# Every second feed-forward of an eight-batch sandwich kernel one step later, with halved rotary products and split preparation waits

## The chip, the cores and the metric

The kernel runs on one core of one Trainium2 chip. The metric is the device time of one execution in microseconds (us), from the first to the last instruction and what lies around it. A profiled execution gives, beside it, the span and what each engine did in it: TensorE (PE, matrix products; PEld its weight loads), VectorE (DVE), ScalarE (ACT), GpSimd (POOL) and SyncE (SP), which here issues the transfers.

## The reference

Eight batches x of 512 tokens by 256 features go through four sub-layers, each with a norm ahead and a norm behind it:

```python
x = x + _layernorm(_L0_attn_ref(_layernorm(x), ...))   # causal attention, 16 heads of 16,
...                                                    # plus one rotary score of 32 common to all heads
x = x + _layernorm(_L0_ffn_ref(_layernorm(x), ...))    # ternary weights, relu squared, hidden 1024
x = x + _layernorm(_L1_attn_ref(_layernorm(x), ...))   # "mixer": cumulative sums of p_w*cos, p_w*sin
x = x + _layernorm(_L1_ffn_ref(_layernorm(x), ...))    # relu, hidden 1024
```

with, in the first attention,

```python
k_rope = _rotary_apply(c_kv @ W_k_rope, cos, sin)
q_rope = _rotary_apply(x @ W_q_rope, cos, sin)
scores = jnp.einsum('bqhd,bkhd->bhqk', q, k)
scores = scores + jnp.einsum('bqr,bkr->bqk', q_rope, k_rope)[:, None]
```

and the ternary weights of the first feed-forward prepared from the latent ones (mean of absolute values, rounding, clipping, a low-rank product added).

## The kernel before, in words

All work of a batch is on one core and the batches overlap. Each engine has its own program, put together from named items. An item is a step such as S (a tile of scores), T (transposes of exponentials), fc (one of 8 products into the hidden layer of the first feed-forward) or gather (products that pick and add mixer terms). The items stand in four chains: a, attention of batches 0 to 7; d, the dense work (first feed-forward `fc`, `fproj`; the mixer's projections `z`, `query`; the mixer's output product `oout`; second feed-forward `gc`, `gproj`); m, the mixer (turn, frac, fold, cos, sin, scan, mix, gather, gate, silu); p, the preparation of weights, once.

Within a chain the order is that of `chains()`; across chains it is written out for each engine in `MERGE`, whose words say how many items of which chain come next (`a8 p a2` is eight of a, one of p, two of a). `PARTS` says which items an engine takes part in. Engines meet by semaphores only: `is_filled` and `is_drained` for banks of PSUM, `need` for other events. An engine that waits holds up all that stands behind it in its own order.

In chain d, for batches 1 to 7, `first_dense_items(b)` is followed by `second_dense_items(b - 1)`, and inside the latter, between gc and gproj, stand the norm and transposes (`head_items(b + 1)`: fstats, fnorm, fxT) of the first feed-forward of the next batch. The short name g(b) is used here for the second feed-forward of batch b: gstats, gnorm, gxT, gc, gproj, gystats, gsum. The banks of PSUM are planned from the orders (`plan_banks`): attention rotates over banks 0 to 2, chain d over 4 to 6, bank 3 is for PV (the product of weights and values), 7 for the mixer's sums and the preparation.

Where the steps are in the code of the profile: on TensorE S is L922, T L930, PV L948, OT (transposes of attention's output) L957, the general `product` L865 (fc with weights wfc, gc with wf, z, query, q, k, rotary qr with wqr and kr with wkr, and `base`, the rotary scores, shown as 32*128), `tokens_out` L875 (out with wo, oout with wout, fproj with wpr, gproj with wf and hid), `half_transposes` L857 (fxT, zxT, gxT), gather L1016, prep L1054 to L1075. On VectorE: drains of scores L1410, rotation L1340, L1341 and L1344, scan L1487, mix L1496, sums x + norm L1332, silu L1505, drains of gproj L1518. On ScalarE: exponentials L1176, copies L1183, statistics (`spread`) L1119, `gsum` scaling L1263, `normed` L1110, cosine and sine L1243 and L1246. On GpSimd: the reciprocal square roots L746, squares of the hidden layer L766, the last sum L786, and ternary weights L803 to L818. On SyncE: the store of the result L728, loads of ratios for the mixer L718.

Buffers that bear on the order: `xnd` holds the normed input of each dense part, and is also where statistics throw their unused output; `x3` holds x + oout and then the result, until it is stored (semaphore `stored`, awaited by osum L1508); `means` keeps the means of four batches.

## Time and profile before

| what | value |
|---|---|
| median of 3 runs | 1410.93 us (1410.14 to 1413.29) |
| the profiled execution | 1407.21 us, its span 1405.4 us |
| granted TensorE clock, mean of the span | 0.949 |
| TensorE busy | 1227.4 us, 87% |
| VectorE busy | 1101.7 us, 78% |
| ScalarE busy | 1054.7 us, 75% |
| GpSimd busy | 336.7 us, 24% |
| chain that ended last, by engine | PE 46%, DVE 21%, ACT 19%, issue 9% |

Busy is time with an instruction under way. A line of the timeline gives the start, the duration of a group of like instructions on that engine, the engine, the line of code, the operation, what is written and read, the tile (128*32 is 128 rows by 32 columns of TensorE) and the count; in brackets stands idle time before it and what ended that. The stretches in the first group of rows are cut at the starts of `out` of batches 0 to 7 (the last product of an attention), and, behind 1171.8, at 1261.4 and at the start of `oout` of batch 7.

### The profile page before, as it was taken

How to read it: one execution, taken by the hardware profiler on the slowest of the kernel's cores; microseconds unless marked ns; L12 is line 12 of the kernel's file. 1: busy time of each engine (PE TensorE's matmuls, PEld its weight loads, DVE VectorE, ACT ScalarE, POOL GpSimd, SP SyncE). 2: the span in 40 equal slices, each digit the busy share in tenths (PEclk: the TensorE clock that was granted, in tenths of full speed). 3: DMA queues.
4: the chain of work that ended last, by engine and by line, in shares of the span. 5: the costliest groups of instructions: out<-in, count | busy, mean ns of one | idle time of the engine just before them, and what ended most of it. 6: DMA issues, size and time to landing. Idle time of an engine off the chain costs nothing.

```text
span 1405.4 us, 22661 instructions
## 1 busy us (share of the span) xinstructions
PE 1227.4 (87%) x7820; PEld 774.3 (55%) x7820; DVE 1101.7 (78%) x2259; ACT 1054.7 (75%) x2107; POOL 336.7 (24%) x317
## 2 busy tenths in 40 slices
PE   5889987888899998999999997998999998874767
PEld 2565664364546565666646764565646755542444
DVE  3683358779988988988888997898788998998940
ACT  4784789689789878798778888597778889547532
POOL 3943203400121303220134001430032201511021
PEclk9799999999999999999999999999999999996879
DMA  8404114412252105520334131511352131103000
GB/s 260 99 13 101 28 24 137 108 50 61 70 135 61 31 1 150 130 53 1 124 80 107 24 100 45 136 31 24 108 124 57 31 92 47 45 19 126 23 16 15
DMA packets 72019, 101.49 MB, mean 72 GB/s; under 512 B 10641, under 2 KB 44065, under 8 KB 71905
## 3 DMA queue, kind: packets, MB, share of 16 engines
q1 hardware_dynamic: 71904, 100.03, 27.2%
q8 instruction: 64, 1.05, 0.3%
q14 instruction: 51, 0.41, 0.1%
HBM read 74.31 MB, written 25.69 MB: 71 GB/s over the span
## 4 chain that ended last, share of the span: by engine, by line
PE 46%; DVE 21%; ACT 19%; issue 9%; DMA 2%; SPq 2%; POOL 1%; DVEq 0%; POOLq 0%; ACTq 0%
PE ps L865 15%; PE ps L875 12%; DVE work L1487 8%; PE ps L930 5%; ACT work L1176 5%; ACT work L1183 3%; PE ps L922 3%; PE ps L948 3%; DVE work L1410 3%; PE ps L1016 3%; DVE work L1496 2%; DVE work L1478 2%; ACT xnd L1119 2%; DVE work L1468 1%; PE ps L857 1%
## 5 line engine op out<-in xcount | busy, mean ns | idle before, releaser
L1487 DVE TENSOR_TENSOR_SCAN work<-work 128x512 f32<-128x512 f32 x256 | 313.2, 1254 | 23.0 <-ACT work L1243 21.0
L1410 DVE CUSTOM_DVE_ANT_0 work<-ps,work 128x384 f32<-128x384 f32 (+3 forms) x512 | 228.9, 486 | 109.9 <-PE ps L922 106.5
L1176 ACT ACTIVATE work<-work 128x384 f32<-128x384 f32 (+3 forms) x512 | 264.4, 560 | 44.9 <-DVE work L1410 44.1
L746 POOL TENSOR_TENSOR later_norms<-later_norms,singles 128x2 f32<-128x2 f32 x112 | 97.0, 867 | 711.6 <-ACT xnd L1119 428.5
L930 PE MATMUL ps<-ident,work 128*128 128x128 f32 x1280 | 202.4, 284 | 23.7 <-ACT work L1183 11.0
L930 PEld LDWEIGHTS ps<-ident,work 128*128 128x128 f32 x1280 | 152.6, 145 | 82.5 <-issue 33.5
L1183 ACT COPY work<-ps 128x512 f32<-128x512 f32 x300 | 170.9, 576 | 8.6 <-PE ps L930 8.3
L1496 DVE TENSOR_TENSOR work<-work 128x1024 f32<-128x1024 f32 x128 | 160.7, 1255 | 4.0
L922 PE MATMUL ps<-work 96*128 96x384 bf16 (+3 forms) x512 | 124.8, 311 | 29.9 <-ACT work L1183 28.0
L865 PE MATMUL ps<-led_xTd,wfc 128*128 128x512 f32 x256 | 122.3, 615 | 0.8 <-ACT led_xTd L1103 0.8
L875 PE MATMUL ps<-wf,hid 128*128 128x256 f32 x512 | 114.1, 383 | 5.5 <-issue 5.5
L875 PE MATMUL ps<-wpr,hid 128*128 128x256 f32 x512 | 114.7, 383 | 4.1 <-POOL hid L766 4.1
L865 PE MATMUL ps<-led_xTd,wf 128*128 128x512 f32 x256 | 115.8, 609 | 1.4 <-issue 1.4
L875 PEld LDWEIGHTS ps<-wf,hid 128*128 128x128 f32 x512 | 97.6, 192 | 21.2 <-issue 8.0
L875 PEld LDWEIGHTS ps<-wpr,hid 128*128 128x128 f32 x512 | 97.1, 192 | 19.2 <-POOL hid L766 5.9
L766 POOL TENSOR_TENSOR hid<-hid 128x512 f32<-128x512 f32 x64 | 79.9, 1258 | 111.7 <-ACT hid L1198 111.5
L1478 DVE SCALAR_TENSOR_TENSOR work<-work,smalls 128x512 f32<-128x512 f32 x128 | 97.3, 804 | 6.0 <-ACT work L1234 3.6
L948 PE MATMUL ps<-work 128*32 128x128 f32 x2560 | 93.4, 284 | 0.4 <-ACT work L1183 0.4
L922 PEld LDWEIGHTS ps<-work 96*128 96x128 bf16 x512 | 43.1, 99 | 84.2 <-ACT work L1183 40.4
L1239 ACT ACTIVATE work<-work 128x1024 f32<-128x1024 f32 x64 | 67.2, 1058 | 26.1 <-DVE work L1478 25.9
L865 PEld LDWEIGHTS ps<-led_xTd,wf 128*128 128x128 f32 x256 | 49.2, 195 | 64.4 <-issue 63.7
L1016 PE MATMUL ps<-work,sel 128*32 128x512 f32 x512 | 63.1, 610 | 19.1 <-DVE work L1496 18.9
(174 smaller groups left out, 1967.4 us busy)
## 6 DMA issues: line engine op xcount, KB each, us to landing
work<-values SPq DMA_DIRECT2D x64, 256.0 KB, 3.3
work<-ratios SPq DMA_DIRECT2D x64, 256.0 KB, 3.3
scratch<-work SPq DMA_DIRECT2D x32, 384.0 KB, 4.5
work<-scratch SPq DMA_DIRECT2D x64, 192.0 KB, 3.9
work<-scratch SPq DMA_DIRECT2D x64, 128.0 KB, 4.2
x_in<-x SPq DMA_DIRECT2D x8, 512.0 KB, 7.0
work<-scratch SPq DMA_DIRECT2D x64, 64.0 KB, 4.3
values<-work SPq DMA_DIRECT2D x16, 256.0 KB, 2.8
```

Of the source, the lines that this page charges most:

```text
L865: i = mm(dst, l, r, start=j == 0, stop=j == len(pairs) - 1)
L875: i = mm(ps[:, bank(b, name), t * D:(t + 1) * D], lhs[:, j, tt * P:(tt + 1) * P], rhs[:, j, :], start=j == 0, stop=j == n_k - 1)
L922: i = mm(out_of(b, name)[:, at:at + nk], stack[0:SROWS, hg % 2, 0, j, qt * P:(qt + 1) * P], stack[0:SROWS, hg % 2, 1, j, 0:nk], start=True ...
L930: i = tr(ps[:, bank(b, name), t * P:(t + 1) * P], sc[:, n % 4, t * P:(t + 1) * P], ident[:])
L948: i = mm(ps[32 * j:32 * j + 32, PV, qt * P:(qt + 1) * P], v_all[:, v0:v0 + 32], pt[:, (hg * UNITS + u) % 6, at + t * P:at + (t + 1) * P], ...
L1016: i = mm(ps[l * W:(l + 1) * W, bank(b, f"mem{quad}"), :], sel[:], ring[:, at, m, :], start=half == 0 and m == 0, stop=half == 1 and m == M ...
L1176: i = s_.activation(part_of, part_of, ACT.Exp, scale=-1.0, bias=nmax[:, row:row + 1])
L1183: s_.copy(pt[:, n % 6, 0:nk], out_of(b, name)[:, 0:nk]).then_inc(*drains(b, name))
L1410: i = v_.tensor_tensor_reduce(sc[:, n % 4, at:at + nk], out_of(b, name)[:, at:at + nk], base_of(qt), -SCORE_SCALE, BIG, ALU.add, ALU.min, ...
L1478: i = v_.scalar_tensor_tensor(ring[:, SIN_HALF[r], m, :], kvr[:, slot, :], turns[:, r, m:m + 1], whole[:, COS_HALF[r], m, :], ALU.mult, AL ...
L1487: v_.tensor_tensor_scan(ring[:, at, m, :], pwr[:, slot, :], ring[:, at, m, :], 0.0, ALU.mult, ALU.add).then_inc(*scanned.one)
L1496: v_.tensor_tensor(both, both, qc[:, half * MH:(half + 1) * MH], ALU.mult).then_inc(*mixed.one)
```

## The change

It has three parts, and a new order of merging (`MERGE`) for all five engines.

*The second feed-forward one step later.* `oout`, its statistics and sums leave `second_dense_items` and become `output_items`. From batch 2 on, chain d is first(b), second(b-2), output(b-1), where it was first(b), second(b-1) with the output at its head. The end is second(6), output(7), second(7). `head_items(b + 3)` goes with it. On ScalarE `gystats` throws its output into `zc`, and so waits for the saved values of batch b+2; `fstats` and `fystats` wait for events of batch b-3 instead of b-2; `means` keeps all eight batches. In TensorE's order, attention 7 ends (`out(7)`) with g(0) to g(3), and the transposes and gc0, gc1 of g(4), done ahead of it. Behind it come the rest of g(4), oout(5), fc to query of batch 7, g(5), oout(6), g(6), oout(7), g(7), with the gathers of the last two mixers among them.

*Halved rotary products.* qr and kr use four column groups of 32 (two halves of the tokens, each with and without the swap), with 256 columns for each instruction. The rotation of q then has 256 elements on 64 partitions, that of k keeps 512 on 64. `base` of the later half is two products.

*Preparation.* The loads are split: the first prepare steps and the ternary weights wait for five of them (`loaded_raw`), the rest for all. In the order prep 8 to 12 are among the scores of attention 0, and 13 to 15 stand ahead of `out(0)` (before: behind `out(0)`, the last of them after kr of batch 1). Dense work starts sooner: fxT of batch 0 directly behind kr of batch 1, six fc of batch 0 ahead of its first score (before: three), and z and query of batch 0 some eight score tiles sooner.

```diff
 def second_dense_items(b):
 
-    return (steps(b, ["oout", ("oystats", 0), ("oystats", 1), ("osum", 0), ("osum", 1), ("gstats", 0), ("gstats", 1), ("gnorm", 0),
-                       ("gxT", 0), ("gnorm", 1), ("gxT", 1)] + [("gc", g) for g in range(HC)]) + head_items(b + 2) +
+    return (steps(b, [("gstats", 0), ("gstats", 1), ("gnorm", 0),
+                       ("gxT", 0), ("gnorm", 1), ("gxT", 1)] + [("gc", g) for g in range(HC)]) + head_items(b + 3) +
             steps(b, [("gproj", 0), ("gystats", 0), ("gsum", 0), ("gproj", 1), ("gystats", 1), ("gsum", 1)]))
+def output_items(b):
+
+    return steps(b, ["oout", ("oystats", 0), ("oystats", 1), ("osum", 0), ("osum", 1)])
...
-    for b in range(1, B):
-        dense += first_dense_items(b) + second_dense_items(b - 1)
+    dense += first_dense_items(1) + output_items(0) + head_items(2)
+    for b in range(2, B):
+        dense += first_dense_items(b) + second_dense_items(b - 2) + output_items(b - 1)
+    dense += second_dense_items(B - 2) + output_items(B - 1)
...
-                    product(b, "qr", out_of(b, "qr")[0:2 * DR],
-                            [(wqr[:, c].rearrange("p s r -> p (s r)"), xa_c[c]) for c in range(DC)])
+                    may_fill(pe, b, "qr")
+                    for c in range(DC):
+                        for g in range(4):
+                            h = g % 2
+                            i = mm(out_of(b, "qr")[g * DR:(g + 1) * DR, 0:T // 2], wqr[:, c, g // 2, :],
+                                   xa_c[c][:, h * T // 2:(h + 1) * T // 2], start=c == 0, stop=c == DC - 1)
+                    i.then_inc(*fills(b, "qr"))
...
-                    product(b, "kr", out_of(b, "kr")[0:2 * DR], [(wkr[:].rearrange("p s r -> p (s r)"), ckv)])
+                    may_fill(pe, b, "kr")
+                    for h in range(2):
+                        for g in range(4):
+                            of = (h + g) % 2
+                            i = mm(out_of(b, "kr")[g * DR:(g + 1) * DR, h * T // 2:(h + 1) * T // 2], wkr[:, g // 2, :],
+                                   ckv[:, of * T // 2:(of + 1) * T // 2], start=True, stop=True)
...
-                    product(b, f"base{n}", out_of(b, f"base{n}")[:, 0:(n + 1) * P],
-                            [(qrope[0:DR, n * P:(n + 1) * P], krope[0:DR, 0:(n + 1) * P])])
+                    name, h = f"base{n}", n // 2
+                    may_fill(pe, b, name)
+                    queries = qrope[h * DR:(h + 1) * DR, n % 2 * P:(n % 2 + 1) * P]
+                    if h == 1:
+                        mm(out_of(b, name)[:, 0:T // 2], queries, krope[DR:2 * DR, T // 2:T], start=True, stop=True)
+                    first, n_key = h * T // 2, (n % 2 + 1) * P
+                    i = mm(out_of(b, name)[:, first:first + n_key], queries, krope[h * DR:(h + 1) * DR, 0:n_key],
+                           start=True, stop=True)
...
                 if n == 0:
-                    pe.wait_ge(loaded, 16 * n_rest[0])
+                    pe.wait_ge(loaded_raw, 16 * n_raw[0])
...
                     if b and n == 0:
-                        is_filled(act, *((b - 2, "gxT1") if b > 1 else (0, "zxT1")))
+                        is_filled(act, *((b - 3, "gxT1") if b > 2 else (b - 1, "zxT1")))
...
                     is_drained(act, b, f"gproj{n}")
-                    spread(2, n, lambda t: xnd[:, t, :], x2[:, b % 2], o_stats)
+                    need(act, kv_saved[1], min(b + 2, B - 1), 1)
+                    spread(2, n, lambda t: xnd[:, t, :], zc[:, 1].rearrange("p (t d) -> p t d", t=2), o_stats)
...
-            def rotate(b, name, dst):
+            def rotate(b, name, dst, n):
+
                 is_filled(dve, b, name)
-                v_.tensor_tensor(rtmp[0:DR, 0, :], out_of(b, name)[0:DR], rope[0:DR, :], ALU.mult)
-                v_.tensor_tensor(rtmp[0:DR, 1, :], out_of(b, name)[DR:2 * DR], rope[DR:2 * DR, :], ALU.mult
+                v_.tensor_tensor(rtmp[0:2 * DR, 0, 0:n], out_of(b, name)[0:2 * DR, 0:n], rope[0:2 * DR, 0:n], ALU.mult)
+                v_.tensor_tensor(rtmp[0:2 * DR, 1, 0:n], out_of(b, name)[2 * DR:4 * DR, 0:n], rope[2 * DR:4 * DR, 0:n], ALU.mult
                                  ).then_inc(*drains(b, name))
```

## Rows read from the trace of the kernel before

**Rows 1.** Stretches: length, then busy (xcount) of PE, PEld, DVE, ACT, POOL; clock.

```profile
0.00:104.40 104.40, 81.64 (x667) 54.23 (x668) 65.00 (x224) 67.16 (x146) 64.47 (x57) 0.89 0.47 125
104.40:228.20 123.80, 113.06 (x809) 73.52 (x808) 60.12 (x196) 88.12 (x195) 24.32 (x29) 0.97 0.26 61
228.20:377.60 149.40, 122.94 (x848) 74.83 (x849) 126.81 (x260) 121.32 (x229) 31.14 (x28) 0.93 0.30 77
377.60:534.60 157.00, 145.25 (x966) 92.78 (x965) 134.70 (x275) 130.11 (x260) 33.20 (x33) 0.98 0.27 67
...
1009.90:1171.80 161.90, 152.39 (x998) 97.86 (x996) 143.05 (x291) 136.59 (x278) 36.60 (x36) 0.98 0.32 86
1171.80:1261.40 89.60, 78.11 (x319) 46.77 (x319) 82.63 (x87) 56.56 (x103) 24.96 (x20) 0.96 0.09 28
1261.40:1351.80 90.40, 54.29 (x198) 29.79 (x196) 77.39 (x82) 55.13 (x89) 7.92 (x8) 0.82 0.20 65
1351.80:1405.40 53.60, 38.09 (x120) 24.90 (x120) 3.14 (x6) 16.74 (x42) 7.82 (x9) 0.82 0.04 15
```

**Rows 2.** TensorE timeline around the end of attention 7: start, us, work.

```profile
1159.13 3.62 PE L875 MATMUL ps<-wout,work 128*128 128x256 f32 x16
...
1168.54 0.66 PE L857 MATMUL ps<-ident,xnd 128*128 128x128 f32 x4 [1.06 <-ACT xnd L1110]
...
1175.69 13.90 PE L865 MATMUL ps<-led_xTd,wf 128*128 128x512 f32 x32
1191.66 1.92 PE L1016 MATMUL ps<-work,sel 128*32 128x512 f32 x16 [2.07 <-DVE work L1496]
...
1196.14 13.98 PE L875 MATMUL ps<-wf,hid 128*128 128x256 f32 x64
```

**Rows 3.** TensorE timeline, tail.

```profile
1292.45 1.93 PE L1016 MATMUL ps<-work,sel 128*32 128x512 f32 x8 [13.33 <-DVE work L1496]
...
1351.82 6.21 PE L875 MATMUL ps<-wout,work 128*128 128x256 f32 x16 [4.36 <-DVE work L1505]
```

**Rows 4.** ScalarE, GpSimd and store queue behind gproj1 of batch 5 (timeline).

```profile
1211.23 0.51 ACT L1119 ACTIVATE x<-xnd,singles 128x256 f32<-128x256 f32 x1 [1.08 <-DVE xnd L1518]
...
1213.14 1.09 ACT L1263 ACTIVATE xnd<-xnd,means,later_norms 128x256 f32<-128x256 f32 x2 [0.82 <-POOL later_norms L746]
...
1214.31 1.79 POOL L786 TENSOR_TENSOR x<-x,xnd 128x512 f32<-128x512 f32 x1 [1.20 <-ACT xnd L1263]
...
1211.76 4.77 SPq L728 DMA_DIRECT2D out<-x  x2
```

**Rows 5.** TensorE timeline: rotary products; transposes ahead of PV and ahead of z.

```profile
21.98 1.93 PE L865 MATMUL ps<-xTa,wqr 128*64 128x512 f32 x4
...
25.75 1.07 PE L865 MATMUL ps<-work,wkr 128*64 128x512 f32 x2
...
1133.60 0.66 PE L930 MATMUL ps<-ident,work 128*128 128x128 f32 x4
1134.19 1.09 PE L948 MATMUL ps<-work 128*32 128x128 f32 x32
...
1135.44 0.60 PE L930 MATMUL ps<-ident,work 128*128 128x128 f32 x4
1135.88 1.45 PE L865 MATMUL ps<-led_xTd,wz 128*128 128x512 f32 x3
```

**Rows 6.** VectorE rotation by line: ns min, median, max; then a 256-element operation.

```profile
L1340 DVE TENSOR_TENSOR work<-ps,rope x16: 668/670/679, 24.0 to 1035.5; 32x512 f32<-32x512 f32 x16
...
L1344 DVE TENSOR_TENSOR work<-work x16: 679/826/1299, 25.4 to 1036.9; 32x512 f32<-32x512 f32 x16
...
L1424 DVE TENSOR_TENSOR xna<-ps,work 128x256 f32<-128x256 f32 x32 | 13.6, 425 | 1.1
```

**Rows 7.** TensorE timeline; VectorE waits, 104.4 to 228.2: total, times, longest.

```profile
28.79 0.76 PE L1054 MATMUL ps<-ident,work 128*16 128x128 f32 x4 [1.96 <-DMA b2r<-b]
...
DVE work L1410 <- PE ps L922: 46.7, 26, 11.7
```

49 lines of the change are left out of this document (30 added, 19 removed), and 87 rows, old and new, of the table MERGE.

## The prediction

> **What bounds the kernel now.** The page comes first. TensorE is busy 87% of a 1405.4 us span, VectorE 78%, ScalarE 75%, and the chain that ended last is spread over all three (PE 46%, DVE 21%, ACT 19%). So no engine alone sets the time, and the question is which stage has which limit. I therefore cut the span at the moments when TensorE starts `out` (L875, wo) of batches 0 to 7, which end one attention each [rows 1]. What to see there: from 377.6 on the five steps take 156 to 163 us each, TensorE busy 145.25 of 157.00 in the first and 152.39 of 161.90 in the last, 93 to 94%: these steps are at TensorE's limit. The step 228.2 to 377.6 has only 122.94 us of TensorE work, because no second feed-forward lies in it, and still takes 149.40 us. The step before it, 104.4 to 228.2, has 113.06 us of work in 123.80. Behind 1171.8, where attention is over, 233.6 us remain with 170.5 us of TensorE work (78.11 + 54.29 + 38.09): there the last two mixers on VectorE set the pace (82.63 of 89.60 us, 77.39 of 90.40 us busy), TensorE waits for them up to 13.33 us at a time [rows 3], and the last 53.6 us are one serial second feed-forward at the granted clock of 0.82.
>
> So work that leaves the steps at TensorE's limit is worth its full time there, and costs in the tail only what doesn't fit into TensorE's gaps.
>
> **Part 1, the second feed-forward (g) one step on.** On TensorE one g is gc, 32 products in 13.90 us, gproj, 64 in 13.98 us, and two groups of four transposes of 0.66 us, 29.2 us in all; `oout` takes 3.62 us [rows 2]. Before, when `out(7)` starts, g(0) to g(4) and the transposes of g(5) are done. After, g(0) to g(3) are done, and of g(4) the transposes and gc0 and gc1. So ahead of `out(7)` there is less by six gc (10.4), gproj (14.0), oout(5) (3.6) and a pair of transposes (1.3): 29.3 us. By steps: the one from 377.6 loses its g altogether and gains nothing; each of the four behind it trades one g for another and stays at TensorE's limit. The step from 377.6 has then some 145.25 - 28 = 117 us of TensorE work and 134.70 of VectorE's. How long does it take? The nearest row is the step before it, also without a g: 149.40 us at 122.94 us of TensorE and 126.81 us of VectorE [rows 1]. Its gain is bounded by nothing (157.0, as now) and by 157.0 - 134.7 = 22.3 us (VectorE's own busy time). I take 9, from 157 to about 148, since the row of the like step is the nearest evidence.
>
> The 29.3 us come back behind `out(7)`, where TensorE now idles 63 us. The order there is g(4), oout(5), fc(7), z and queries of 7, g(5), oout(6), g(6), oout(7), g(7). Three places decide. First, mixer(7) can begin only after fc, fproj and z of batch 7. Gathers of batch 6 waited up to 2.07 us for VectorE [rows 2], so TensorE is nearly even with it, and gather and oout(5) now lie ahead: about +3. Second, g(5) and most of g(6) fill gaps like the 13.33 us one ahead of the first gather of batch 7, the 4.36 us one ahead of oout(7) [rows 3]; nearly free, and TensorE then stays at its higher clock: oout(7) took 6.21 us behind idle time, in a stretch of granted clock 0.82, against 3.62 for oout(5) [rows 1 to 3], so -2.6. Third, the end: gproj1(6), 7 us, is now behind the last gather and directly ahead of oout(7), and the statistics of oout(7) on ScalarE wait for the sum of g(6), because both use the buffer `xnd`. That sum comes late after gproj1: statistics from 1211.23, scaling from 1213.14, the sum on GpSimd until 1216.10, for a product that ended at 1210.1, so 6.0 us [rows 2, 4]. Against that the 4.36 us wait for silu and the first half of oout(7) run meanwhile. And the sum x + oout(6) on VectorE waits until the result of batch 5 is stored (two stores took 4.77 us, 2.4 each [rows 4]), with scans of mixer 7 queued behind it. I take +10 for the third (7 - 4.4 for gproj1 that isn't hidden, 3.7 for the wait on VectorE, the rest for statistics and steps between). Together +3 - 2.6 + 10 = **+10 to +11**; bounds 0 (only the first and the second) and +29 (nothing fits).
>
> Every g issues also its part on the other engines and on SyncE: the store of its result is queued behind loads for the mixer of batch 7 or ahead of them. The stores are 2.4 us each and the queue has them far apart; I take 0, and up to 2.4 us each where a load of ratios stands behind one. The new wait of `gystats`, for the saved values of a batch two further, is one for an event half a step old, and costs 0; behind it on ScalarE are exponentials of attention, so it would be seen at once if it did not.
>
> **Part 2, rotary products.** Before, qr takes 1.93 us (four products of 512 columns in a 128x64 tile) and kr 1.07 us [rows 5]. After, there are 16 instructions of 256 columns, or 8, in 128x32 tiles of four column groups. The nearest row is the gather, 16 products of 512 columns in 128x32 tiles in 1.92 us [rows 2], so 0.12 us each; with half the columns 16 take 1.0 us, and 8 of kr 0.5 to 1.0. `base` gains two products of 256 columns, 0.2 to 0.5 us. Net -0.5 to -1.0 us for each batch on TensorE; for the range, nothing gained at all. On VectorE, q's three operations over 512 elements, 0.67 us for each product and 0.83 for the sum, become three over 256, which take 0.43 us each by a like operation [rows 6]: -0.9 us each batch. As VectorE is not the limit of the middle steps only TensorE's part counts: -1.0 us a step at most, five times, taken as -0.9 each.
> In this case's trace a switch of tile mode shows so: four transposes ahead of a PV take 0.59 us from start to start, four ahead of a full product 0.44 [rows 5], 0.15 us more. The Trainium skill, "TensorEngine Tiling (Array Packing)", Key Properties, says against this part that changing the tiling mode drains TensorE. The rows agree in sign, but qr and kr had a mode of their own before as well, so by the rule too nothing is added but in `base`.
>
> **Part 3, preparation.** Before, TensorE idles 1.96 us ahead of 28.79 for the last of the loads [rows 7]; the first two prepare steps now wait for five loads only and this goes: -2 in the first stretch. Steps 8 to 12 move from the end of attention 0 into its middle, where TensorE is idle a fifth of the time (81.64 of 104.40 us [rows 1]), steps 13 to 15 ahead of `out(0)`; these are 1.90, 1.90 and 2.00 us of TensorE work behind 104.4 and leave that step: -5.8, and come in part into the first (+3, against -3 for the earlier ones). In the step from 104.4 VectorE waits 46.7 us for scores from TensorE, the longest 11.67 us while fc(0) runs first [rows 7]. Transposes of the first feed-forward start some 5 us sooner, but six fc stand ahead of the first score instead of three (+4 there, back later, as they are not in the loop's way). I take -2 and -8 for the two stretches; bounds 0 and -6, and 0 and -14. The projections of batch 0 come some 8 score units sooner, so mixer(0) starts 16 to 20 us sooner; that is worth 2 us in the step from 228.2, where VectorE has 126.81 of 149.40 us, with bounds 0 and -8.
>
> **The sum.** First stretch -2, second -8, third -2, fourth -9, four steps of -1.2 (rotary, and oout no longer beside the projections of attention) about -5: -26 at `out(7)`, of 35 us of work that is gone from there. Tail +11. Net -15: the profiled span 1405.4 becomes 1390. The profiled execution took 1407.2, 3.7 us less than the median of the runs, 1410.93; by the same difference **1396 us**. Its own range: -25 to -5, so 1386 to 1406.
>
> **The rivals.**
> B, all of it is collected. The fourth step falls to about VectorE's limit (157 to 141, -16), the third by 4, the tail costs 8 as gproj1(6) ends before silu does: -2 - 8 - 4 - 16 - 5 + 8 = -27, **1384** (1374 to 1390). For it: 134.7 us of VectorE in the fourth step; against: the third step has still more slack and doesn't use it [rows 1].
> C, the steps are bound by the chain score, exponential, transpose, and not by TensorE's amount. Then the fourth step keeps its 157 and the second gives 4: -2 - 4 - 1 - 1 - 4 + 11 = -1, **1410**. For it: 149.40 us at 122.94. Against: five steps alike, at 93 to 94%, and 7 us less for the step without g. The Trainium skill, "Perfetto Trace Analysis", Identifying the Most-Contended Engine, speaks for C: matmul busy share is not a good measure of TensorE's headroom, weight-load busy share is better; that is 92.78 of 157.00 us in the fourth step [rows 1], 59%.
> D, slower. In the steps of batches 3 to 7 `oout` of one batch now stands directly behind gproj1 of the batch before. Its statistics on ScalarE wait for the 6.0 us chain to that sum [rows 4]; `oout`'s two banks are not free until the sums are drained, and fc0 or fc1 on TensorE needs one. Before, `oout` stood ahead of the gc of its own batch, far from the gproj1 before it. What lies between now is `oout`, 3.6 us. If ScalarE and then TensorE stand for more than 3.3 us in each of five steps (+16.5) the -15 is gone; at the whole 6 us with what the store adds, 6.5 each, it is -15 + 32 = +17; the likely one is +4.5 each, +22 - 15 = +7, **1418**. For it: no slack in the middle steps. Against: the order puts score units between, and attention has three score banks of its own.
> E, the change does not do what it says: parts 2 and 3 alone, -10 and -5 with g's shift costing what it gives: -15, lies in A's range and is no case of its own.
>
> **How the numbers follow.** A 0.52 (1396), B 0.22 (1384), C 0.12 (1410), D 0.14 (1418). A measurement of this kernel can tell about 0.2% of 1410.93, 2.8 us, from no change: faster is below 1408.1, slower above 1413.8. A is faster nearly always (0.50, 0.02 same), B always; of C a half is same, 0.05 faster, 0.01 slower; D 0.11 slower, 0.01 same, 0.02 faster. So faster 0.79, same 0.09, slower 0.12. The range of 1376 to 1414 leaves out the lower fifth of B and the most of D.
>
> **What would show it.** Right: the start of `out(7)` at about 1146 instead of 1171.8; the step of batch 2 to 3 at 145 to 150 us with 117 us of TensorE work; four steps of 155 to 161; a first gather of batch 7 with no long idle ahead of it; oout(7) in 3.6 us; about 244 us from `out(7)` to the end instead of 233.6; qr near 1.0 us; no idle for a load at 27 us. Wrong: idle of TensorE for ScalarE or GpSimd behind each `oout`, steps above 160 (D); a fourth step of 155 or more (C). The weakest term is the tail's +11: it is made of small waits that no row shows yet.

## The result, and the profile after

The changed kernel took 1416.79 us (median of 8 runs, 1413.12 to 1421.85), the kernel before beside it 1411.25 us (8 runs, 1405.84 to 1414.65): a ratio of 1.0048, interval 1.0031 to 1.0066. It is half a per cent **slower**; the forecast was 1396 us. The profiled execution took 1413.55 us, its span is 1411.7 us, at a mean granted clock of 0.949, as before.

The same cuts as in [rows 1], at the starts of `out(0)` to `out(7)` (now L889), then at 1270, at the start of `oout(7)` and at the end. Columns: length, busy time (xcount) of PE, PEld, DVE, ACT and POOL, granted clock, DMA share, GB/s.

```profile
0.00:105.80 105.80, 79.25 (x720) 55.41 (x721) 64.51 (x224) 68.26 (x149) 64.79 (x57) 0.92 0.47 125
105.80:231.80 126.00, 107.12 (x815) 70.09 (x813) 71.33 (x207) 95.97 (x203) 28.96 (x31) 0.97 0.32 81
231.80:375.70 143.90, 122.17 (x895) 77.80 (x895) 127.19 (x271) 119.31 (x232) 27.89 (x27) 0.94 0.30 78
375.70:517.20 141.50, 120.05 (x883) 75.32 (x883) 117.00 (x253) 109.16 (x219) 27.36 (x27) 0.95 0.28 69
...
993.10:1155.20 162.10, 149.74 (x1010) 95.16 (x1011) 136.35 (x272) 135.85 (x264) 31.45 (x32) 0.98 0.27 71
1155.20:1270.00 114.80, 87.08 (x343) 52.07 (x341) 91.16 (x106) 68.62 (x134) 26.06 (x24) 0.90 0.17 56
1270.00:1356.80 86.80, 74.28 (x284) 44.65 (x285) 67.01 (x66) 52.85 (x90) 10.53 (x10) 0.89 0.09 28
1356.80:1411.70 54.90, 36.27 (x121) 23.33 (x119) 3.83 (x7) 18.92 (x48) 8.68 (x10) 0.85 0.04 15
```

Against [rows 1], stretch by stretch (forecast in brackets): first +1.5 (-2), second +2.2 (-8), third -5.5 (-2), fourth, the one without a g, 157.0 to 141.5, -15.5 (-9). The four steps behind it took 637.2 us and now take 638.0, +0.8 (-5). So `out(7)` starts at 1155.2 instead of 1171.8: -16.6 instead of -26. Behind it 233.6 us became 256.5: **+22.9** instead of +11. What is won up to there is more than given back in the tail.

Where the tail grew shows between marks of TensorE's timeline, counted from `out(7)`:

| from `out(7)` to | before | after | grown by |
|---|---|---|---|
| first projection of batch 7 | 79.7 | 85.7 | +6.0 |
| first gather of batch 7 | 120.7 | 132.5 | +5.8 |
| last gather | 173.8 | 192.7 | +7.1 |
| `oout(7)` | 180.0 | 201.6 | +2.7 |
| end | 233.6 | 256.5 | +1.3 |

The view of waits (who waited for whom) of the kernel after has three groups that the one before did not have: TensorE's scores for the loads of the scratch buffer, the gate (L1537) for the load of the divisors, `osum` (L1366) for the store of an older result. Of the 21.8 us on the scratch buffer 12.4 lie ahead of `out(3)`, 9.7 of them ahead of the very first score, and 9.4 in the four steps behind it. Columns: engine, line, waited for; total us, times, longest.

```profile
PE ps L954 <- DMA work<-scratch: 21.8, 8, 9.7
DVE x L1366 <- DMA out<-x: 17.4, 5, 6.7
DVE work L1537 <- DMA work<-rates: 16.4, 5, 5.9
```

The chain that ended last (start, us, what) runs through two of them around `oout(6)`:

```profile
1289.58 17.48 PE ps L889 x80
...
1307.12 0.54 SPq L736
...
1308.40 0.55 SPq L730
...
1309.00 4.24 DMA out<-x
1313.27 0.89 DVE x L1366 x2
1314.17 2.18 ACT xnd L1152 x8
```

The 80 products are gproj(5) and `oout(6)`. SyncE may load the next divisors (L736) only when `oout` has read the buffer they go to, and the second half of batch 5's store stands behind that load; the landing takes 4.24 us, and only then may `osum` overwrite the same buffer. The chain names SyncE's queue, but the queue cost almost nothing here: the sum that is stored was ready on GpSimd only at 1308.89, 0.1 us ahead of the store.

```profile
1307.61 1.28 POOL L798 TENSOR_TENSOR x<-x,xnd 128x512 f32<-128x512 f32 x1 [1.20 <-ACT xnd L1297]
```

TensorE's side of it, in its timeline:

```profile
1306.98 1.92 PE L1048 MATMUL ps<-work,sel 128*32 128x512 f32 x16
1317.21 1.12 PE L871 MATMUL ps<-ident,xnd 128*128 128x128 f32 x4 [8.31 <-ACT xnd L1143]
1319.81 1.12 PE L871 MATMUL ps<-ident,xnd 128*128 128x128 f32 x4 [1.48 <-ACT xnd L1143]
...
1356.81 3.62 PE L889 MATMUL ps<-wout,work 128*128 128x256 f32 x16
1368.38 1.12 PE L871 MATMUL ps<-ident,xnd 128*128 128x128 f32 x4 [7.96 <-ACT xnd L1143]
```

`oout(7)` takes 3.62 us, not 6.21 [rows 3], as forecast.

### The profile page after: what moved, and what is told of

Its sections match the earlier page's. It is cut to its first block, busy times and chain, and to the rows that moved or that the text cites. A ratio compares the mean times of both kernels' runs of the same rounds, so it can differ in the third digit from the quotient of the medians.

```text
span 1411.7 us, 23164 instructions
## 1 busy us (share of the span) xinstructions
PE 1213.8 (86%) x8060; PEld 773.2 (55%) x8060; DVE 1094.4 (78%) x2259; ACT 1062.6 (75%) x2111; POOL 324.1 (23%) x317
## 4 chain that ended last, share of the span: by engine, by line
PE 46%; ACT 17%; DVE 14%; DMA 7%; issue 7%; POOL 4%; SPq 3%; POOLq 0%; DVEq 0%; ACTq 0%
PE ps L889 16%; PE ps L879 14%; PE ps L962 5%; ACT work L1210 4%; DVE work L1523 4%; PE ps L954 3%; PE ps L980 3%; DVE work L1446 3%; ACT work L1217 3%; DMA work<-scratch 3%; DMA scratch<-work 2%; PE ps L1048 2%; ACT xnd L1152 2%; SPq L648 1%; POOL work L767 1%
## 5 line engine op out<-in xcount | busy, mean ns | idle before, releaser
L1523 DVE TENSOR_TENSOR_SCAN work<-work 128x512 f32<-128x512 f32 x256 | 315.4, 1262 | 26.2 <-ACT work L1277 23.7
L758 POOL TENSOR_TENSOR later_norms<-later_norms,singles 128x2 f32<-128x2 f32 x112 | 92.2, 824 | 648.6 <-ACT xnd L1152 335.3
L962 PE MATMUL ps<-ident,work 128*128 128x128 f32 x1280 | 200.7, 282 | 24.3 <-DVE work L1446 11.9
L954 PE MATMUL ps<-work 96*128 96x384 bf16 (+3 forms) x512 | 125.7, 313 | 43.9 <-DMA work<-scratch 21.8
L879 PE MATMUL ps<-led_xTd,wf 128*128 128x512 f32 x256 | 124.5, 632 | 2.2 <-issue 2.2
L889 PE MATMUL ps<-wpr,hid 128*128 128x256 f32 x512 | 113.7, 381 | 5.3 <-POOL hid L778 5.3
L889 PE MATMUL ps<-wf,hid 128*128 128x256 f32 x512 | 113.3, 381 | 1.6 <-issue 1.6
L889 PEld LDWEIGHTS ps<-wpr,hid 128*128 128x128 f32 x512 | 96.6, 190 | 20.0 <-POOL hid L778 6.9
L889 PEld LDWEIGHTS ps<-wf,hid 128*128 128x128 f32 x512 | 96.4, 190 | 17.8 <-issue 5.1
L778 POOL TENSOR_TENSOR hid<-hid 128x512 f32<-128x512 f32 x64 | 73.9, 1158 | 128.3 <-ACT hid L1232 128.1
L1293 ACT ACTIVATE hid<-ps,smalls 128x512 f32<-128x512 f32 x64 | 43.9, 687 | 52.7 <-PE ps L879 52.3
L879 PEld LDWEIGHTS ps<-led_xTd,wfc 128*128 128x128 f32 x256 | 48.2, 198 | 59.0 <-issue 46.3
```

The source lines that it names most:

```text
L758: g_.tensor_tensor(rstds[chain][:, tokens], spreads[chain][:, tokens], power[:, tokens], ALU.pow).then_inc(*rstd.one)
L879: i = mm(dst, l, r, start=j == 0, stop=j == len(pairs) - 1)
L889: i = mm(ps[:, bank(b, name), t * D:(t + 1) * D], lhs[:, j, tt * P:(tt + 1) * P], rhs[:, j, :], start=j == 0, stop=j == n_k - 1)
L954: i = mm(out_of(b, name)[:, at:at + nk], stack[0:SROWS, hg % 2, 0, j, qt * P:(qt + 1) * P], stack[0:SROWS, hg % 2, 1, j, 0:nk], start=True ...
L962: i = tr(ps[:, bank(b, name), t * P:(t + 1) * P], sc[:, n % 4, t * P:(t + 1) * P], ident[:])
L1523: v_.tensor_tensor_scan(ring[:, at, m, :], pwr[:, slot, :], ring[:, at, m, :], 0.0, ALU.mult, ALU.add).then_inc(*scanned.one)
```

## The experiments

Eighteen kernels. "After" is the changed kernel, "before" the one before; a ratio is that to the kernel before, measured beside the run. "Middle steps" are those from the start of `out(3)` to that of `out(7)`, "the tail" all that follows. A theory's number in an expectation is explained there or here: the last ones set co-critical chains (several engines' chains of like length, so that a cut on one engine only shows the next) against delays that are fixed by the order of work and its landings.

Kernels 6 to 8 and 11 to 17 were executed once each. How far one execution can be trusted shows in the kernels whose work is that of after in the stretch compared: in eight of them (after, 4, 5, 6, 7, 9, 10, 16) the middle steps took 635.9 to 640.8 us; the tail took 256.5 us in after and 259.1 in 4, where nothing was changed in it. So a difference under some 3 us in a stretch of one profile is not told from none. The profile of after is also a good one in the fourth stretch: 141.5 us, where 4 and 9 took 141.2 and 141.7 and six others with the same work 144.3 to 144.9.

**1. `oout` ahead of gproj1.** Is it D's place that costs? On TensorE `oout` of batches 1 to 6 moves ahead of gproj of the batch before; on SyncE the load of divisors moves ahead of the store.

```diff
+    mover, ahead, lag = {"pe": ("oout", "gproj", 1), "sp": ("inv", "gsum", 2)}[engine]
+    for b in range(1, B - 1) if engine == "pe" else range(2, B):
...
+            order.insert(to, order.pop(at))
```

> The changed kernel with one thing moved: on TensorE, oout of batches 1 to 6 stands ahead of gproj of the batch before (it was directly behind), with the PSUM banks planned to match, and on SyncE the load of the mixer's divisors (inv), which waits for that oout, ahead of the store of the older result. ScalarE and VectorE keep their order but for the drain of gproj0, which is taken sooner on VectorE for batches 0 to 3. Theory 1 (the loss is the place of oout: in the changed kernel the gate on VectorE waited 5.67 and 5.86 us for inv in the tail, 16.4 us in all, because inv may be overwritten only when oout has read it): the waits of the gate for the load vanish, the tail from out(7) to the end falls from 256.5 us by 8 to 12, and the kernel takes 1403 to 1409 instead of 1416.8. Theory 2 (the tail is long because 29 us of TensorE work were put into it, and the waits for inv only stand where VectorE would wait for something else): at most -2, 1415 to 1417. Theory 3 (the second wait for one bank makes gproj1 and fc0 late): slower, 1418 to 1424.

Measured: 1438.81 us, ratio 1.0205 (1.0162 to 1.0248), slower than after and than every theory said. Middle steps 654.5 us, tail 263.4. The gates no longer wait for divisors; they wait for TensorE's gathers instead (14.1 us in ten waits; 6.5 in after), TensorE's `product` waits 13.6 us for banks that sums on VectorE drain (11.0 in after), and the sums' wait for stores is still there (17.9 us). The edit also gives gproj1 another bank, so it says only that this order is no cure, not what D's wait costs.

**2 and 3. The rotary products, taken out of after and put alone into before.**

```diff
-                    may_fill(pe, b, "qr")
-                    for c in range(DC):
-                        for g in range(4):
...
+                    product(b, "qr", out_of(b, "qr")[0:2 * DR],
+                            [(wqr[:, c].rearrange("p s r -> p (s r)"), xa_c[c]) for c in range(DC)])
```

> The changed kernel with the rotary products as before (qr of 4 products in 128x64 tiles, kr of 2, rotation of 512 elements on 32 partitions); orders and waits unchanged. By the prediction (TensorE -0.5 to -1.0 us a batch in steps at TensorE's limit, VectorE -0.9): 2 to 6 us slower than the changed kernel, 1419 to 1423. Rival, that tile modes and 48 more instructions a batch cost what the halves save: no difference, 1416 to 1418. Rival, that they are the cause of the loss: faster, 1411 or below.

> The kernel before with the halved rotary products alone; orders and waits of before. By the prediction: -3 to -6, so 1405 to 1408. Rival, that the rotary part gives nothing in this kernel because the projections wait for the pieces of q and k to be sent anyway: 1410 to 1412. Together with the kernel without them it says whether this part is worth the same in both orders.

After without them: 1431.85 us, ratio 1.0156 (1.0116 to 1.0197). Before with them: 1408.41 us (10 runs), 0.9986 (0.9963 to 1.0010), no difference that can be told; in its profile `out(0)` to `out(7)` takes 1065.0 us instead of 1067.4, while `out(0)` comes 3.1 us later (TensorE waits until 32.54 for the last load, in before until 28.79) and the tail takes 236.3 us. So they are worth some 2 us in the old order, not told from nothing, and about 15 in the new, far above the 2 to 6 expected. In the new order more is lost than TensorE's own share: the middle steps take 645.6 us at 596.86 us of TensorE work, after takes 638.0 at 587.55. Why the new order is so much more sensitive isn't shown.

```profile
525.60:1171.20 645.60, 596.86 (x3884) 376.16 (x3885) 555.79 (x1129) 528.75 (x1043) 127.97 (x131) 0.97 0.28 74
```

**4. Preparation waits for all loads again,** in after's order.

```diff
-        loaded_raw = sem("loaded_raw")
+        loaded_raw = loaded_ident
...
-                pe.wait_ge(loaded_raw, 16 * n_raw[0])
+                pe.wait_ge(loaded, 16 * n_rest[0])
```

> The changed kernel with the preparation waiting for all loads again (one semaphore, as before), orders unchanged. By the prediction the split wait is worth the 1.96 us gap of TensorE at 28.8 us, so 1 to 2 us slower than the changed kernel if that reaches out(0), with out(0) at 107 to 108 instead of 105.8. Rival, that the ternary weights on GpSimd (they end at about 78 us before) set when prepare steps can run and so out(0): up to 6 us slower. Rival, hidden: no difference.

Measured: 1424.31 us, 1.0110 (1.0064 to 1.0156). `out(0)` starts at 116.05 instead of 105.81; the rest takes 1306.9 us against 1305.9. GpSimd's timeline shows why: its first preparation now stands in the queue ahead of batch 0's pieces (L767) and waits 21.46 us for the last load.

```profile
29.35 0.53 POOL L816 MEMSET work<- 128x512 f32 x1 [21.46 <-DMA b2r<-b]
...
33.97 0.61 POOL L767 CAST work<-xna 128x512 bf16<-128x512 f32 x1 [0.27 <-DVE xna L1392]
```

By these profiles the split wait is worth 10 us in this order, all in the first stretch; by the medians (1424.31 against 1416.79) 7.5.

**5 and 6. The two waits around `oout` in the tail taken away by other buffers:** the gated output of batches 5 and 6 no longer overwrites the divisors, and (5 only) x + oout(6) goes to a buffer of its own, so that `osum(6)` waits only for the store of batch 4 and `osum(7)` only for that of batch 5.

```diff
+        gated = [inv] * (B - 3) + [work[:, stack_at + i * 1024:stack_at + (i + 1) * 1024].rearrange("p (r t) -> p r t", r=RH)
+                                   for i in range(2)] + [inv]
+        def x3_of(b):
+
+            return xna if b == B - 2 else x3
...
-                    need(dve, stored, b - 1, 2)
+                    need(dve, stored, b - 1 - (b >= B - 2), 2)
```

> The changed kernel, complete, with two waits of the tail taken away by other buffers: the mixer's output of batches 5 and 6 goes to memory that attention 7 has left (so the divisors of batches 6 and 7 are loaded when silu is done and not when oout is, and stand ahead of the store in SyncE's order), and x + oout of batch 6 goes to a second buffer (so it waits for no store). Theory 1 (in the tail a chain of small waits around oout is the loss: the gate waited 5.67 and 5.86 us for the divisors, the sum of oout 0.9 and 6.7 us for a store): both gone, fc1 of batch 7 starts 3 to 4 us sooner, oout(7) follows at once on its statistics, the tail from out(7) to the end is 247 to 251 instead of 256.5 us, the kernel at 1408 to 1411 against 1416.8. Theory 2 (the tail is bound by three second feed-forwards one behind the other, each some 50 us from its norm to the norm of the next, of which the waits for the load lie beside): the gates' waits vanish, the tail falls by no more than 3 us.

> As the kernel with both buffers, but only the mixer's output has another place; x + oout of batch 6 still waits for the store. Theory 1: about half of what both give, 3 to 5 us, seen at fc1 of batch 7 and at the gates. Theory 2: 0 to 2 us.

Measured: 1416.34 us (10 runs), 1.0048 (1.0023 to 1.0074), tail 259.2 in a profile of 1420.36 us, the slowest of the ten; and 1418.77 us, tail 256.4. The two gates of the tail waited 11.5 us for divisors; now they wait 4.84 and 3.20 us for TensorE's gathers, and VectorE waits 3.67 us for a gproj:

```profile
1205.40 0.69 DVE L1551 TENSOR_TENSOR work<-ps,work 128x512 f32<-128x512 f32 x1 [4.84 <-PE ps L1062]
```

```profile
1354.91 0.69 DVE L1568 TENSOR_TENSOR xnd<-ps,b2r 128x512 f32<-128x512 f32 x1 [3.67 <-PE ps L903]
```

The gates' wait lies on the chain and is worth **nothing** that these runs can tell: of its 11.5 us 8.0 are left, now for TensorE, which stands right behind it. And `osum(7)` stays idle for 6.37 us in 5, though nothing in that kernel makes it wait for the store of batch 6. The profile puts the wait to that store, which lands at 1370.94; but the norm that `osum(7)` needs ends on GpSimd at 1370.83.

```profile
1370.12 0.71 POOL L772 TENSOR_TENSOR later_norms<-later_norms,singles 128x2 f32<-128x2 f32 x1 [1.19 <-ACT xnd L1166]
1370.93 0.88 DVE L1380 SCALAR_TENSOR_TENSOR x<-ps,later_norms,x 128x256 f32<-128x256 f32 x2 [6.37 <-DMA out<-xna]
```

In after the same norm ends at 1363.97 and `osum(7)` starts at 1364.44: of its 6.74 us of idle time the store explains 0.5. Before, it was idle for 5.79 us, for the norm alone. Counted like this, of the 17.4 us in five waits for stores only 6.6 lie behind the norm.

**7 and 8. Seven eighths of gproj(5) left out,** in after and in before.

```diff
+                if tag == "gproj" and b in (5,):
+                    n_k = 1
```

> The changed kernel, with seven eighths of gproj of batch 5 left out (8 products in place of 64, 12.2 us less of TensorE; the result of batch 5 is not the reference's). The prediction's view (g(5) fills TensorE's gaps in the tail): 0 to 3 us less. The rival (g(5), g(6) and g(7) stand in one chain behind the queries of batch 7): the whole 12 us less in the tail, 244 instead of 256.5 us.

> The kernel before with the same left out of gproj of batch 5, which there stands ahead of fc of batch 7, beside mixer 6. If TensorE and VectorE are even there: 3 to 8 us less of the 233.6 us tail; if it is hidden beside the mixer: 0 to 2. Beside the same cut in the changed kernel it tells what a second feed-forward costs at either place.

Measured: 1421.01 and 1408.18 us, tails 256.4 and 237.0. In after the first half of `oout(6)` starts 12.2 us sooner (136.1 against 148.2 behind `out(7)`), its second half, which waits 4.75 us for VectorE's drain of gproj(5), at 142.7, and the last gather 0.5 us sooner. In before the tail was not shorter either (237.0 against 233.6). The time of gproj ahead of `oout(6)` isn't what makes the tail long.

**9 and 10. Another order in the tail.** 9: on ScalarE g(5)'s statistics and scaling stand behind the sines of batch 7, and `silu(7)` behind gc(6). 10: besides, 5's buffers, gproj(6) behind the last gather on TensorE, and its sum later on VectorE.

```diff
+    if engine == "act":
+        put(order, [(last - 2, "gstats", 0), (last - 2, "gstats", 1), (last - 2, "gnorm", 0), (last - 2, "gxT", 0),
+                    (last - 2, "gnorm", 1), (last - 2, "gxT", 1)], (last, "sin", 1))
+        put(order, [(last, "silu", 0)], (last - 1, "gc", 7))
+    if engine == "pe":
+        put(order, [(last, "gather", 3)], (last - 1, "gc", 7))
```

> The changed kernel, complete, with ScalarE's order alone altered in the tail: the statistics, norm and transposed copies of g(5) stand behind the first sines of mixer 7 instead of ahead of its first cosines, and the tanh of mixer 7 ahead of the statistics and scaling of gproj0(6). Leaving 12 us of TensorE work out of g(5) had moved the tail by nothing (256.4 against 256.5 us), so neither TensorE's load nor a chain of three feed-forwards sets it. Theory 3 (the tail is set by mixer 7 on VectorE, and what lengthens it is g's part on ScalarE, queued ahead of the waves: VectorE waited 6.46 us for the first cosine, 3.5 us for tanh): the wait for the first cosine falls to about 2 us as before, tail 256.5 less 4 to 7, so 250 to 253, the kernel 1410 to 1413. If ScalarE is not it: tail within 2 us of 256.5.

> Complete too: the same order on ScalarE, both buffers of the tail kernel (divisors and x + oout of batch 6 without their waits), the last gather of mixer 7 ahead of gproj0(6) on TensorE, and the drain of gproj0(6) behind silu on VectorE. Theory 3 (the waits of mixer 7 on VectorE add up: 6.5 and 1.3 us for ScalarE, 5.9 for the divisors, 1.9 and 1.3 for TensorE, 3.5 for tanh; each one removed alone is taken by the next): tail 242 to 247 instead of 256.5, kernel 1402 to 1408. If the second feed-forwards are the longer chain once mixer 7 is freed: 248 to 253.

Measured: 1423.52 us, 1.0091 (1.0062 to 1.0119), tail 264.6; 1425.70 us, 1.0098 (1.0067 to 1.0130), tail 266.9. In 9 the first gather of batch 7 comes 7.3 us later, 139.8 behind `out(7)`, since on TensorE it stands behind gc(5), whose transposes now wait for ScalarE:

```profile
1274.25 1.11 PE L894 MATMUL ps<-ident,xnd 128*128 128x128 f32 x4 [16.49 <-ACT xnd L1166]
```

Taking ScalarE's work out of the mixer's way puts it in TensorE's. In 10 the last gather waits 5.59 us for VectorE and gproj(6) has nothing beside it:

```profile
1355.95 3.64 PE L1090 MATMUL ps<-work,sel 128*32 128x512 f32 x16 [5.59 <-DVE work L1574]
1359.52 14.19 PE L931 MATMUL ps<-wf,hid 128*128 128x256 f32 x64
1373.55 3.62 PE L931 MATMUL ps<-wout,work 128*128 128x256 f32 x16
```

**11 and 12. Less TensorE work in the middle steps.** Seven eighths of four gproj are left out, of batches 0 to 3 in after, 1 to 4 in before (the edit of 7 with other batches): 4 x 13.98 x 7/8 = 48.9 us at the 13.98 us of [rows 2].

> The changed kernel with seven eighths of gproj of batches 0 to 3 left out (12.2 us less of TensorE in each of the four steps between out(3) and out(7), results of these batches not the reference's). By the prediction these steps are at TensorE's limit: each falls by 10 to 12 us, 40 to 49 in all of 638.0. Rival (they are set by ScalarE and VectorE in attention's loop, TensorE's 90% is a consequence): 0 to 15 in all.

> The kernel before with the same left out of gproj of batches 1 to 4, which there lie in the same four steps, between out(3) and out(7) (637.2 us). By the prediction 40 to 49 us less; by the rival 0 to 15. If before falls more than the changed kernel, its steps were nearer to TensorE's limit than those of the changed one.

Measured: 1422.33 and 1408.86 us, once each. The middle steps of before, of before with the cut, of after and of after with the cut:

```profile
534.60:1171.80 637.20, 594.00 (x3902) 377.49 (x3900) 551.88 (x1132) 519.52 (x1049) 142.91 (x135) 0.98 0.30 78
```

```profile
534.20:1172.40 638.20, 551.77 (x3677) 335.55 (x3675) 551.57 (x1132) 520.07 (x1050) 143.92 (x135) 0.95 0.30 78
```

```profile
517.20:1155.20 638.00, 587.55 (x4004) 374.55 (x4005) 552.33 (x1129) 529.46 (x1043) 129.84 (x131) 0.98 0.29 75
```

```profile
522.70:1161.00 638.30, 556.27 (x3780) 340.57 (x3781) 551.76 (x1129) 528.77 (x1043) 130.35 (x131) 0.94 0.29 75
```

TensorE's busy time falls by 42.2 us and by 31.3 us, and the steps take 1.0 and 0.3 us **more**, that is the same. At 93% busy these steps are not at TensorE's limit. Part of the cut is given back at once: the granted clock falls from 0.98 to 0.95 and 0.94.

**13 to 15. Less work for VectorE or ScalarE alone.** Half of each mix of all batches is left out (in after, in before), and half of each cosine and sine (in after).

```diff
-                    v_.tensor_tensor(both, both, qc[:, half * MH:(half + 1) * MH], ALU.mult).then_inc(*mixed.one)
+                    v_.tensor_tensor(both[:, 0:1], both[:, 0:1], qc[:, half * MH:half * MH + 1], ALU.mult).then_inc(*mixed.one)
...
-                    cos = ring[:, COS_HALF[n]]
+                    cos = ring[:, COS_HALF[n], 0:1]
```

> The changed kernel with half of each mixing product on VectorE left out (128x512 in place of 128x1024, about 0.6 us each, 16 a batch: 9 to 10 us less of VectorE per batch; the mixer's values not the reference's). 42 us less of TensorE work had moved the four middle steps by nothing. If VectorE's load is what sets a step (it is busy 88 to 91% there): each of the four steps 8 to 10 us shorter, 32 to 40 in all of 638.0, and the tail 10 to 20 shorter (two mixers). If the steps are set by the chain score, drain, exponential, transpose inside attention's loop and the written order, not by any engine's load: under 12 in all of the four.

> The same left out of the kernel before. VectorE's load: 32 to 40 us less in the four middle steps (637.2) and 10 to 20 in the tail (233.6); the order: under 12 and, since its tail runs at VectorE's pace with 86 to 92% busy, 10 to 20.

> The changed kernel with half of each cosine and sine on ScalarE left out (128x512 in place of 128x1024, about 0.5 us each, 16 a batch: 8 to 9 us less of ScalarE per batch). If ScalarE's load sets the steps (busy 81 to 85% there): 25 to 35 us less in the four middle steps. Otherwise under 10. In the tail, where VectorE waited 6.5 us for the first cosine: 3 to 8 less.

Measured: 1413.98, 1398.18 and 1420.72 us, a single execution each. Middle steps 635.8 at 519.4 us of VectorE work (33 less), 633.3 at 518.5 (33 less), 641.3 at 504.0 us of ScalarE work (25 less); tails 256.3, 229.3 (against 233.6) and 259.8. In after neither is worth anything beyond 2 us in 638, which a single execution doesn't tell from nothing; in before VectorE is worth some 4 in the middle and 4 in the tail.

**16. g(5) thin.** Its statistics, scaling, gc, relu, gproj and sums work on a few columns only.

```diff
+                    if b == 5:
+                        spread(2, n, lambda t: x3[:, t, 0:16], xnd[:, :, 0:16], o_stats)
+                        return
...
+                    w = 64 if b == 5 else T
```

> The changed kernel with the whole of g(5) made thin: statistics, norm and scaling over 16 of 256 columns, gc and its relu over 64 of 512, gproj with an eighth of its products (result of batch 5 not the reference's); every instruction, wait and its place in each order is kept. TensorE's part of g(5) alone had been free in the tail. If g(5) costs through ScalarE (some 10 us less there, most of it ahead of mixer 7's waves and gathers): the tail 256.5 less 5 to 12. If only places and waits count, not durations: 0 to 3.

Measured: 1416.82 us, tail 255.7. From the first projection of batch 7 to its first gather now 42.0 us instead of 46.8, nearly before's 41.0: this is the +5.8 of the table. It has two parts. One is g(5)'s work on ScalarE ahead of the first cosine of batch 7. In after's timelines:

```profile
1263.80 0.51 ACT L1152 ACTIVATE xnd<-x,singles 128x256 f32<-128x256 f32 x1
...
1265.78 0.90 ACT L1143 ACTIVATE xnd<-x,later_norms 128x256 f32<-128x256 f32 x2
1266.70 1.28 ACT L1277 ACT_TABLE_LOAD   x1
1267.99 1.15 ACT L1277 ACTIVATE work<-work,singles 128x1024 f32<-128x1024 f32 x1
```

```profile
1269.17 2.34 DVE L1523 TENSOR_TENSOR_SCAN work<-work 128x512 f32<-128x512 f32 x2 [6.46 <-ACT work L1277]
```

The first scan of batch 7 waits 6.46 us (L1523). In before's timeline it waits 2.17 us:

```profile
1275.90 2.34 DVE L1487 TENSOR_TENSOR_SCAN work<-work 128x512 f32<-128x512 f32 x2 [2.17 <-ACT work L1243]
```

The other part is TensorE's own order. The fourth mix of batch 7, the last that the first gather needs, ends at 1284.76 on VectorE; the gather starts at 1287.66, as gc(5) stands ahead of it and runs until then:

```profile
1283.53 1.23 DVE L1532 TENSOR_TENSOR work<-work 128x1024 f32<-128x1024 f32 x1
1272.31 15.42 PE L879 MATMUL ps<-led_xTd,wf 128*128 128x512 f32 x32 [0.72 <-issue]
1287.66 1.92 PE L1048 MATMUL ps<-work,sel 128*32 128x512 f32 x16
```

So 2.9 us of the 5.8 are gc(5) on TensorE and the rest is a later fourth mix; in 16, where both are thin, the gather waits 1.73 us for VectorE again. Yet g(5) made thin brings 0.8 us at the end of the tail: of the 2.5 us that the first gather gains against `out(7)` the last has 1.2 left.

**17. All cuts at once:** 11, 13, 15 and 16 in one kernel.

> The changed kernel with all of these cuts at once: seven eighths of gproj of batches 0 to 3 and 5, half of each mixing product, half of each cosine and sine, g(5) thin. Alone, the cut on TensorE, the one on VectorE and the one on ScalarE each left the four middle steps at 635.8 to 641.3 us (638.0) and the tail at 255.7 to 259.8 (256.5). Theory 4 (several chains of nearly the same length run through the three engines, so that what is saved on one is lost to the next): together they save what none saves alone, 25 to 45 us of the four steps and 10 to 20 of the tail. Theory 5 (durations don't count, only fixed delays between engines and the written order): under 10 and under 5.

Measured: 1393.02 us. Middle steps 625.3 us, tail 249.3.

```profile
516.60:1141.90 625.30, 549.39 (x3780) 337.08 (x3781) 519.36 (x1130) 503.21 (x1043) 125.68 (x131) 0.96 0.29 76
```

Alone the cuts moved the middle steps by +0.3 (TensorE), -2.2 (VectorE) and +3.3 us (ScalarE); together by -12.7, out of 38, 33 and 26 us less busy time; the tail went from 256.5 to 249.3 us. So there are co-critical chains, and beside them much that no engine's amount of work moves.

**18. Rotary products and the split wait in the old order of g.** A complete kernel: all of 3, and of the preparation only the wait for its own loads, not its move to other places. The diff to before is the rotary part of the change with

```diff
-                pe.wait_ge(loaded, 16 * n_rest[0])
+                pe.wait_ge(loaded_raw, 16 * n_raw[0])
```

and the same wait on the other three engines.

> The kernel before, complete, with the halved rotary products and the split wait of the preparation, and without the second feed-forward's shift and without new orders. The rotary part alone had given a ratio of 0.9986 (0.9963 to 1.0010). If the two parts add what the traces show for them (rotary 2.4 us between out(0) and out(7), the wait for the last load up to 2 us, more in executions where the loads land late): ratio 0.996 to 0.998. If they are hidden as the other savings are: 0.998 to 1.000.

Measured: **1400.68 us** (6 runs, 1398.13 to 1405.33), ratio 0.9937 (0.9913 to 0.9960): faster than both. Preparation's first transposes start at 25.43 with no idle time ahead instead of 28.79 [rows 7]:

```profile
24.43 1.07 PE L917 MATMUL ps<-work,wkr 128*32 128x256 f32 x16
25.43 0.60 PE L1078 MATMUL ps<-ident,work 128*16 128x128 f32 x4
```

`out(0)` starts at 102.3 (before 104.4), `out(7)` at 1163.0 (1171.8), the tail is 233.3 (233.6). This is more than either theory expected (0.996 at best): 2.0 us ahead of `out(0)` and 6.7 between it and `out(7)`, where the rotary products alone had shown 2.4. The profile is of the fastest of the six executions. One reason for more shows in 3: the wait that the split takes away varies with the landing of the loads, 1.96 us in before's profile and 6.44 in that of 3. For the 6.7 us no run shows the reason.

## Why the prediction was wrong

**"These steps are at TensorE's limit"** is the premise that failed, and with it the rule drawn from it, that work which leaves these steps "is worth its full time there, and costs in the tail only what doesn't fit into TensorE's gaps". The forecast of the span was 1390 us and it was 1411.7. The 21.4 us between them add up so: tail +11.9, second stretch +10.2, the four middle steps +5.8, first stretch +3.5, third and fourth -3.5 and -6.5. The largest term lies where the second half of the rule was used.

42 us less TensorE work in before's middle steps left them at 638.2 us (12). The forecast took 93% busy for a limit and wrote down part 1 and part 2 in TensorE's microseconds; the four steps should have fallen by 5 and rose by 0.8. The Trainium skill, "Perfetto Trace Analysis", Identifying the Most-Contended Engine, calls matmul busy share a poor measure of TensorE's headroom and points to that of weight loads. The trace agrees: matmuls were busy 93% and weight loads 377.49 of 637.20 us, 59%, and the cut brought nothing. The prediction had that rule, under rival C, and gave C 0.12. Half of C's premise, that TensorE's amount doesn't bind, was right; its chain was not shown, and its numbers were not right: the fourth step did not keep 157 us. It lost a whole g, on ScalarE (130.11 to 109.16 us), VectorE (134.70 to 117.00) and TensorE together, and fell by 15.5 in this profile, by 12.1 to 12.7 in six kernels with the same work: more than the 9 taken, less than B's 16. As in 17, taking from several engines at once moves a step that none moves alone. What exactly sets the 141.5 us isn't shown.

**The first three stretches,** -2, -8, -2 forecast, +1.5, +2.2, -5.5 measured. The idle at the load went, as forecast, and the split wait is worth 7.5 to 10 us in this order (4). The order itself lost it again: in before's order the same wait brought `out(0)` 2.1 us forward (18), in after's order 1.5 back, with steps 13 to 15 in front of it: from the first score (44.63; before 45.66, in 18 43.02) to `out(0)` it takes 61.2 us, against 58.7 and 59.3. In the second stretch the first score comes 3.9 us sooner (32.5 us behind `out(0)` instead of 36.4), but from there to `out(1)` it takes 93.5 us instead of 87.5: VectorE's work in the stretch rose from 60.12 to 71.33 us and ScalarE's from 88.12 to 95.97, since mixer 0 came forward into it. The prediction counted this only as a gain for the third stretch, where it did appear. That the extra work is what lengthened the second stretch is argued, not shown.

**Part 2, rotary.** qr was put at 1.0 us and took 1.07; kr at 0.5 to 1.0 and took 1.07, no change from [rows 5], since it too makes 16 records, not 8. The `base` products took 27.2 us in all instead of 25.0, 0.3 more a batch.

```profile
118.12 1.07 PE L913 MATMUL ps<-xTa,wqr 128*32 128x256 f32 x16
119.12 1.99 PE L879 MATMUL ps<-work,wku 128*128 128x512 f32 x4
121.04 1.07 PE L925 MATMUL ps<-work,wkr 128*32 128x256 f32 x16
```

That is -0.6 us a batch, inside the stated 0.5 to 1.0 and below the 0.9 used. Its worth in the whole was not right: 2.4 us from `out(0)` to `out(7)` in the old order (one profile), about 15 in the new (2), against the 4.5 taken (five steps of 0.9).

**The tail,** +10 to +11 forecast, +22.9 measured: the largest miss, and mis-sized in each of its three places. (1) Batch 7's projections: "about +3" for gather and `oout(5)` ahead of them was +6.0. One of the causes stands in the timeline: `oout(5)`'s bank is drained late, as `osum` on VectorE stands behind a gate that waits for divisors, and fc(7) waits 3.95 us for the bank (2.52 in 5, where the gate doesn't wait for divisors).

```profile
1194.87 1.92 PE L1048 MATMUL ps<-work,sel 128*32 128x512 f32 x16
1200.74 12.78 PE L879 MATMUL ps<-led_xTd,wfc 128*128 128x512 f32 x22 [3.95 <-DVEq L1370]
```

```profile
1197.78 0.69 DVE L1537 TENSOR_TENSOR work<-ps,work 128x512 f32<-128x512 f32 x1 [5.67 <-DMA work<-rates]
```

(2) "g(5) and most of g(6) fill gaps; nearly free" looked at the sum of TensorE's idle time alone. It cost +5.8 ahead of the first gather, of which 16 gives back 4.8: TensorE had the time, but gc(5) stood in front of the gather in its order (2.9 us), and on ScalarE, which feeds both g and the mixer, g(5) stood ahead of the cosines. The 13.33 us gap that gc(5) was to fill was a wait of the very gather that it then delayed. (3) Between first and last gather, +7.1 where the forecast had nothing. TensorE's run there (gathers, gproj(5), `oout(6)`, sum, store, statistics, gc(6), gproj0(6)) and VectorE's mixes seem to be of like length: neither the gates' waits (5, 6) nor gproj(5) (7) nor VectorE's mixes (13) alone shorten the tail, all cuts together shorten it by 7.2 (17). That is argued from what didn't help; no run isolates this stretch. The end, put at +10 with gproj1(6), sum and store, was +2.7 + 1.3. gproj1(6) had cover from the silu: the silu ends at 1355.39 and `oout(7)` starts at 1356.81. The stores, put at 3.7 for `osum(6)`, cost that sum 0.87 us and `osum(7)` 0.5. So of the tail's terms the first was 3.0 too small, the end (+10 less the 2.6 of `oout(7)`) 3.4 too large, and the two that stood at nothing were 5.8 and 7.1. The 2.4 us for each store were misread as well: [rows 4] give SyncE's issues of two stores from the first to the end of the second, not their landings; that the median landing of a store is 2.2 us in the profile before is luck.

**D** gave 1418, very near the 1416.79 measured, but not for its reason: that is luck. Its waits exist. `osum` waits 17.4 us for stores, but 6.6 of these at most are the store's own; TensorE's `product` waits 11.0 us in five waits for banks that `osum` drains, 4.3 of them in the middle steps, where D took 4.5 in each of five steps; and the link that it missed, divisors behind `oout`, holds the gates for 16.4 us. Yet the middle steps, where D put most of its price of 22 us, lost 0.8 us against before, and the loss is in the tail. Taking the gates' and the sums' waits away in the tail gained nothing (5); in the middle steps the gates' was taken away only with another order of TensorE (1), which was worse. So D's price is refuted by the middle steps as a whole, and what its waits cost there by themselves isn't shown.

**Which part cost.** Rotary and split wait alone: 0.9937. With g one step on and preparation moved as well: 1.0048. The new order as a whole therefore costs 1.1%, some 16 us; how much of it is g's shift and how much the preparation and the first mixer moved forward was not run apart. The parts that were worth keeping were the two small ones.

**Open:** what sets the length of the middle steps. 31 to 42 us less for TensorE, 33 for VectorE, 25 for ScalarE each bring at most 4 us in 638, all together 12.7. Chains of like length on three engines explain the difference between the sum and the parts, the rest may be the fixed run from score to transpose (C's) or landings of the scratch loads (TensorE waits 9.4 us for them in after's middle steps, and not at all in before's, which are as long); no run took these apart.

## What to carry to other kernels

Before a stage's time is written down as an engine's work, cut that engine's work there in one throw-away kernel: a busy share of 93% was no limit, and such a run costs less than a reordering. Work moved into gaps must find a gap on every engine that it uses, and in each queue at the place where it will stand; here places on ScalarE and TensorE itself cost what TensorE's gap gave. A wait in the profile is worth only what no other wait ends just behind it: look when the next input was ready before building a kernel without it (11.5 us of waits for divisors, 8.0 left when they were gone). Try the parts of a compound change alone: two small ones gained 0.6%, the rest lost more than that.
